# Capacity experts: order of marks, slot reads, weighing and the first expert's products

## What is computed

```python
cap = math.ceil(n_tok / n_exp * CAPACITY_FACTOR)            # 4096 / 8 = 512
topk_vals, topk_idx = jax.lax.top_k(weights_flat, TOP_K)     # two experts of a token
sorted_indices = jnp.argsort(-expert_mask, axis=0)[:cap]     # an expert's first 512 tokens
inputs = x_flat[used_idx] * sorted_mask...                   # gathered rows
h = jax.nn.relu(jnp.einsum('ceh,ehi->cei', inputs, experts_inter))
out = jnp.einsum('cei,eih->ceh', h, experts_out) * in_w[..., None]
combined = jnp.zeros_like(x_flat).at[used_idx].add(out.reshape(-1, hidden))
combined = combined + x_flat * (noop_w * noop_mask)[:, None]
```

## Time and profile before

| | us |
|---|---|
| median of three runs | 2871.42 |
| the profiled execution, its own time | 2877.28 |
| its span in the trace | 2875.5 |
| TensorE busy in the span | 2357.5 (82%) |
| VectorE busy | 2047.4 (71%) |
| ScalarE busy | 1841.8 (64%) |
| GpSimd busy | 928.1 (32%) |
| mean granted TensorE clock, share of full speed | 0.908 |

### The profile page before, as it was taken

The page is one execution under the profiler, slowest core; times in us unless marked ns, Lnnn a source line. Parts: engine busy times, 40 slices in busy tenths (PEclk is TensorE's granted clock), DMA queues, the critical chain, the costliest instruction groups (busy, mean ns, idle before and its releaser), DMA issues. The chain is left out here.

```text
span 2875.5 us, 44593 instructions
## 1 busy us (share of the span) xinstructions
PE 2357.5 (82%) x13383; PEld 1207.3 (42%) x13383; DVE 2047.4 (71%) x5859; ACT 1841.8 (64%) x4699; POOL 928.1 (32%) x1259
## 2 busy tenths in 40 slices
PE   3667765838888878599999999997958888888888
PEld 3345544512222236344444444444424444444453
DVE  4526544769999957666666666665778999998855
ACT  2123313327777774477777777776559999999955
POOL 2442255354344333500000000003734444444427
PEclk9778677659999997799999999999979999999979
DMA  6320322022323300000000000000011111111001
GB/s 189 96 76 8 100 77 80 1 43 58 72 49 69 63 12 1 31 1 1 1 1 1 1 1 1 1 1 1 1 35 30 30 30 30 31 30 31 1 1 30
DMA packets 227661, 94.65 MB, mean 33 GB/s; under 512 B 175778, under 2 KB 215522, under 8 KB 227426
## 3 DMA queue, kind: packets, MB, share of 16 engines
q1 hardware_dynamic: 218592, 82.61, 12.1%
q0 software_dynamic: 3584, 7.58, 1.0%
q10 hardware_dynamic: 5250, 1.62, 0.3%
HBM read 30.66 MB, written 19.17 MB: 17 GB/s over the span
## 5 line engine op out<-in xcount | busy, mean ns | idle before, releaser
L2562 ACT ACTIVATE s_pT<-s_ps_t 128x512 f32<-128x512 f32 x1024 | 625.8, 639 | 142.3 <-PE s_ps_t L2150 124.0
L2310 DVE TENSOR_REDUCE s_neg_max<-s_ps_a 128x1 f32<-128x512 f32 x1024 | 666.3, 682 | 63.7 <-PE s_ps_a L2116 53.8
L2553 ACT ACTIVATE s_first<-s_ps_a,s_neg_max 128x512 f32<-128x512 f32 x512 | 391.0, 764 | 24.7 <-DVE s_neg_max L2310 23.2
L2162 PE MATMUL s_ps_t<-ident,s_first 128*128 128x128 f32 x2048 | 317.5, 285 | 82.1 <-ACT s_pT L2562 69.5
L2894 DVE CUSTOM_DVE_ANT_0 s_e<-s_ps_a,w_alibi 128x128 f32<-128x128 f32 (+3 forms) x512 | 231.2, 489 | 187.0 <-PE s_ps_a L2739 186.8
L2481 POOL TENSOR_SCALAR s_first<-s_first,s_rec 128x512 f32<-128x512 f32 x128 | 232.1, 1813 | 368.1 <-DVE s_rec L2316 362.1
L3010 ACT ACTIVATE s_e<-s_e,s_neg_max 128x128 f32<-128x128 f32 (+3 forms) x512 | 283.0, 556 | 42.4 <-DVE s_neg_max L2894 40.9
L2116 PE MATMUL s_ps_a<-s_lanesT 64*128 64x512 bf16 x1024 | 275.4, 401 | 38.8 <-DMA s_lanesT<-n_lanes 22.1
L2162 PEld LDWEIGHTS s_ps_t<-ident,s_first 128*128 128x128 f32 x2048 | 221.3, 142 | 181.8 <-ACT s_pT L2562 140.4
L2180 PE MATMUL s_ps_o<-s_pT,n_v_pad 128*32 128x512 f32 x2048 | 278.9, 618 | 12.2 <-ACT s_oT L2568 12.2
L3020 ACT ACTIVATE s_pT<-s_ps_t 128x512 f32<-128x512 f32 (+3 forms) x512 | 195.5, 434 | 123.1 <-PE s_ps_t L2751 122.8
(11 more groups left out here) (423 smaller groups left out, 4121.4 us busy)
## 6 DMA issues: line engine op xcount, KB each, us to landing
s_y_rows<-s_zeros SPq DMA_DIRECT2D x4, 2048.0 KB, 10.7
s_parts<-s_y_rows SPq DMA_DIRECT2D x32, 256.0 KB, 4.0
s_token_rows<-s_rows SPq DMA_DIRECT2D x4, 1088.0 KB, 5.7
s_Wi<-L_ffn_experts_inter SPq DMA_DIRECT2D x2, 1792.0 KB
x<-L_attn_x SPq DMA_DIRECT2D x4, 512.0 KB, 8.1
out<-x SPq DMA_DIRECT2D x8, 256.0 KB, 2.3
s_lanesT<-n_lanes SPq DMA_TRANSPOSE x64, 4.6
s_shiftedT<-n_lanes SPq DMA_TRANSPOSE x64, 2.4
```

What stands on the lines that cost most here:

```text
L2162: last = pe.transpose(st[n % NK][:, t * P:(t + 1) * P], first[:, p % NF, 2 * t + a, i * P:(i + 1) * P], G.ident[:])
L2310: dve.tensor_reduce(neg_max[:, column(n):column(n) + 1], sa[n % NA][:], AX.X, ALU.max, negate=True).then_inc(s.max_ready, 1)
L2553: act.activation(first[:, g % NF, n % PU, :], sa[n % NA][:], ACT.Exp, bias=neg_max[:, n:n + 1], accum_out=sum1[:, n % (NR * PU):n % (NR * ...
L2562: act.activation(pT[:, n % NP, :], st[n % NK][:], ACT.Exp).then_inc(s.probs_ready, 1)
```

## The change

Three programs of the same block are reordered; no instruction is added or removed.

```diff
 (TensorE)
                 find_slots(2)
-                stir(pe, G, up[0][:], 8)
+                stir(pe, G, up[0][:], 4)
+                find_slots(3)
+                stir(pe, G, up[0][:], 4)
                 turn(0)
-                find_slots(3)
+                upward(0)
                 turn(1)
-                upward(0)
                 for e in range(E):
                     if e + 4 < E:
                         find_slots(e + 4)
+                    if e == 0:
+                        downward(0)
                     if e + 2 < E:
                         turn(e + 2)
                     if e + 1 < E:
                         upward(e + 1)
-                    downward(e)
+                    if e:
+                        downward(e)
 (VectorE)
                 read_slots(2)
+                mark(4)
                 read_slots(3)
                 dve.wait_ge(s.xn_ready, NT)
                 do(dve.tensor_copy(noop[:], rows[:, :, D + E]))
                 for e in range(E):
-                    if e + 4 < E:
-                        mark(e + 4)
-                    weigh(e)
+                    if e + 5 < E:
+                        mark(e + 5)
                     if e + 4 < E:
                         read_slots(e + 4)
+                    weigh(e)
 (ScalarE)
                 copy_xT(0)
+                hide(0)
                 copy_xT(1)
-                hide(0)
```

## The result

The changed kernel takes 2825.72 us, the median of four runs (2819.26, 2823.17, 2828.27 and 2834.70), against 2871.28 for four runs of the kernel before: ratio 0.9846, interval 0.9822 to 0.9869. It is faster, by 45.6 us where 38.9 were forecast, and the median lies 2.3 us under the range. The profiled execution took 2834.70 us, 42.6 less than the profiled one of before. Its shares hardly tell what happened: with the same instructions TensorE is 18.3 us less busy than before, and the others are as they were.

What follows compares the result with a forecast made beforehand. The prediction took a ring over VectorE and TensorE, closed by the mark, as the bound, with GpSimd's queue next. Gains of 20.2 us in pass 1 and 18.7 in pass 2, 38.9 off 2871.42, gave 2832.5 us, range 2828 to 2848.

Steps and rivals of the forecast that it cites:

- What bounds the kernel: Expert loop: VectorE and TensorE wait for each other in a ring closed by the mark, 16.9 us a round; GpSimd slack.
- B: Expert loop: ring not opened, find_slots still held behind a weighing; only 12.4 us gained in all, 2859; chance 0.05.
- C: Expert products: TensorE never gets back to 2.4 GHz, so the kernel is slower, 2910; chance 0.02.
- no change: Whole kernel: nothing gained, needing the ring still closed and a late upward(0); chance 0.03.
- Start: Head of pass 1: find_slots(3) at 95.9, upward(0) at 100.3 lasting 5.5 us, bounds 3.6 and 6.3.
- TensorE's ring: TensorE's products in pass 1: no wait for marks, weigh(0) at 111.0 instead of 117.23, weigh(1) at 123.3.
- GpSimd: Gathers and scatters: marks hold some issues; from scatter(0) at 113.2 its queue bounds, gather(6)'s last issue at 143.5.
- End: Behind pass 1's last turn: no clock fall ahead of upward(5), 25.6 us instead of 28.28, last scatter ends 171.7.
- Rival A: TensorE's gaps ahead of upward(3), (4), (5): clock falls cost 5.8 us a pass; gain 27, 2844; chance 0.16.
- VectorE: VectorE's new order: mark(4) delays read_slots(3) to 102.5, slot reads wait ahead of weighings; none of it costs anything.
- The sum: Both passes: 20.2 and 18.7 us gained, 38.9 in all, taken from the median 2871.42 for 2832.5.
- 3 to 4 of scatter between medians: Last term of the range: 3 to 4 us for scatter, giving 2828 as its low end and 2848 as its high.

Runs made afterwards that it cites:

- c2: Changed kernel with slots read behind the weighing again, as in the kernel before, marks still early: 2825.68 us, ratio 0.9873.
- d1: Changed kernel with stirs (products nobody reads) added at the ends of the attention layers ahead: 2820.19 us, ratio 0.9885.
- d3: Changed kernel with stirs at the ends of the attention layers and 12 more ahead of turn(5) in each expert pass: 2822.14 us, ratio 0.9879.
- a1: Changed kernel unaltered, measured again: 2838.26 us, ratio 0.9891 to the kernel before.
- c1: Changed kernel unaltered, measured a third time, on another chip: 2833.83 us, ratio 0.9896 to the kernel before.
- c3: Changed kernel with downward(0) back behind turn(2) and upward(1), all else changed: 2853.06 us, ratio 0.9960.
- d2: Kernel before with stirs added at the ends of the attention layers ahead: 2855.19 us, ratio 0.9988.
- b1: Changed kernel with 12 more stirs at the head of each of four routings: 2838.93 us, ratio 0.9921.
- b2: Kernel before with 12 more stirs at the head of each of four routings: 2869.47 us, ratio 1.0031.
- b3: Changed kernel with slots read behind the weighing again, marks still early, one run: 2856.71 us.
- b4: Changed kernel with downward(0) back behind turn(2) and upward(1), one run: 2857.90 us.

## Why the prediction was right in its mechanism and wrong in its range

**What bounds the kernel** was right. The ring closed by the mark was opened, and GpSimd's queue took its place as the bound. Rivals B, C and no change are refuted by the timeline: no wait for a mark is left in the loop, and in pass 1 all upward products but one took 3.6 or 3.7 us.

**Start.** find_slots(3) came at 96.94 instead of 95.9, but the first gather was also 0.97 later in this execution. upward(0) went at 100.00 (forecast 100.3) and took 3.70, not 5.5: the clock was up already (1.00 from 101 to 104 us). In other executions (c2, d1, d3) it took 6.1, inside the bounds either way, and the passes were no longer for it. The length that I chose with so much care has no weight, because scatter(0) waits for gather(3) and not for weigh(0).

**TensorE's ring.** weigh(0) came at 109.06 for 111.0, since upward(0) was shorter. weigh(1) came at 124.88 for 123.3: turn(3) waited 2.07 us for its last quarter [timeline of TensorE above]. I never set the landing of gather(3) against turn(3). By my own numbers (issue at 112.0, landing 2.60 later at 114.6, turn(3) at 115.6) there was 1 us of room and no wait. The room went in three parts: turn(3) came early, at 114.81, the last issue of gather(3) late, at 113.59, and the quarter was turned 3.83 us behind that issue, at 117.42. Why the landing took 1.2 longer there than the 2.5 to 2.7 of the other waited-for quarters is open.

**GpSimd.** The holds came as forecast: 1.81 at 100.59, and for mark(5) 1.31 and 1.82. Only mark(6)'s, which I had put upon scatter(0), fell upon gather(3) at 111.47, since weigh(0) was earlier; this made gather(3) later and with it turn(3). Then scatter(0) 114.84 for 113.2, gather(4) 119.97 for 119.3, scatter(1) 125.84 for 124.35 and the last issue of gather(6) 145.12 for 143.5: less the 0.97 of the later start each is within 0.7. L1010 took 1205 to 1219 ns in all its 14 instances, beside gathers or not. By the rule of the Trainium skill ("SBUF — State Buffer", Who interferes with whom) the later of the two is blocked, whichever it is. The traces agree where GpSimd is the later (1.82 for 0.94) and show no L1010 held where it is the later: the one at 90.85, with an issue in course since 89.94, took 1.21.

**End.** I took no fall of the clock ahead of upward(5), and there was none, 3.60. It fell one expert earlier, upward(4) took 6.45, and this was hidden: downward(3) ended at 147.67, and the last quarter of gather(6) was turned at 147.84, 2.72 behind its issue. From that turn to the end of the last scatter, 173.25, are 25.4 us, forecast 25.6. In a1 the fall did come ahead of upward(5) (5.30), in c1 ahead of upward(4) (5.11), and in c1's second pass there was none: one kernel, three forms. Rival A had its mechanism right, but not its price. A fall ahead of upward(4) is hidden by the gathers, and one ahead of upward(5) costs at most the 1.7 by which a1's was longer than 3.60, not the 5.8 of the rival.

**VectorE** was right: no wait of its new order was long enough to reach anything, and the slots read ahead of the weighing gained nothing, as c2 shows. That downward(0) ahead of turn(2) and upward(1) makes the first weighing 3.9 us earlier was right as well (4.4 at scatter(0), by c3); I had not followed this through gather(4) and turn(4) back to TensorE, where it becomes 8 to 10 us.

**The sum.** Over the two passes 37.4 us in the first pair of profiles, for 38.9. Set against 2871.28 that gives 2833.8, and the median of all 16 runs of the changed kernel is 2835.1. So some 8 of the 45.6 us are not of the passes, and by these numbers they were luck. The step that failed is the last term of the range, "3 to 4 of scatter between medians", and with it the baseline that everything outside the passes was tied to. I had both from three runs that lie 3.6 us apart; by their times they are of the slower of two kinds. Two stretches that the change does not touch, the last layer and the routing of pass 2, come in two lengths each, 14 and 7 us apart, by TensorE's clock at their head. A third, the eighth layer, took from 783.4 to 789.7 us in the traces. The runs of one and the same kernel lie 25 us apart, and the three medians of the changed kernel 12.5. The sign was there to be seen in the trace of before: stretches of an untouched layer in which TensorE was busy all the time at a clock of 0.50. With 10 for that term, an estimate from those medians, the range would have begun at 2828 + 3.5 - 10 = 2821.5 and held the result.

## What to carry to other kernels

When two engines wait for each other in a loop, look for what closes the ring: here a product of VectorE that was made one step too late, and a first result that stood behind two others' work. Then write out the queue of the engine that was slack, for it is the next bound, and set each landing against its reader.

Before giving a range, look in the untouched layers for stretches that are busy at the low clock level. Each is a length that can turn out either way in the next run, and three runs that agree don't exclude it.

## What was not expected of the hardware

- TensorE, busy without a break, stayed at its low level for 20 us and more (0.50 from 2780 to 2800 us in the kernel before) with transposes, 8-column products and the two stirs of each batch between them, and ran the same work at the high level throughout when it came in at that level (1.00 in d2). Twelve stirs more at the head of the routing brought it up (b1, b2: last layer 90.8 and 90.7 us). With stirs in the layer ahead it was high in all three traces (d1 to d3), without them in three of twelve.
- On one chip TensorE stopped inside a row of products for 0.2 to 1.1 us at a time with nothing that the profile shows as the cause (b1, b3, b4), 1.6 to 3.3 us in each pass that had them. It isn't settled what it was.
